# Splitting the first exponential of an attention chunk in two, so that the next projection waits for one bank

## The chip, the cores and the metric

The kernel runs on one core of one Trainium2 chip. The metric is the device time of one execution in microseconds (us). The core's engines run side by side, each through its own queue of instructions, and are ordered by semaphores alone: TensorE (PE; its weight loads are listed as PEld), ScalarE (ACT), VectorE (DVE), GpSimd (POOL) and SyncE (SP), which issues the DMAs here.

## The reference

One block of a perceiver, for four batches of 256 rows of width 256, in float32. Three steps, each added to its input: cross attention (16 heads of 64) of the rows on a context of 4096 keys of width 192; a gated linear recurrence; a mixture of eight experts, of which each row takes two. The change lies in the cross attention:

```python
q = (x @ Wq).reshape(b, n, h, d).transpose(0, 2, 1, 3)
k = (context @ Wk).reshape(b, -1, h, d).transpose(0, 2, 1, 3)
v = (context @ Wv).reshape(b, -1, h, d).transpose(0, 2, 1, 3)
sim = jnp.einsum('bhid,bhjd->bhij', q, k) * scale
attn = jax.nn.softmax(sim, axis=-1)
out = jnp.einsum('bhij,bhjd->bhid', attn, v)
```

## The kernel before, in words

**Pairs, quads, chunks.** Two heads (a pair) are worked on at once, one in each half of the 128 partitions; two pairs are a quad. There are 16 quads (four batches of four). A pair's 4096 keys are taken in 8 chunks of 512 (numbered s = 0 to 7), so a quad has 16 chunks (t = 0 to 15), and the whole cross attention 256. `CHUNK` gives their order and `T` numbers them from the start.

**What TensorE does in a chunk**, in the order of its queue (`quad` of `nc.Block.tensor`, from L386 on): for s = 0 the row maxima (`row_max`, L328) and the next pair's queries (`project_q`, L270); for some s a "guess" (L307), two matmuls of the next pair's scores in rough precision, from which DVE takes a maximum (`chunk_max`, L597); the chunk's scores, in two halves of 12 matmuls (L315, `hf` = 0 and 1), added onto banks which ACT has filled with the negated row maxima (`seed`, L482); in every s but 0 another guess; then one projection job out of a list written by hand (`JOBS`): 18 matmuls for keys (`project_k`, L279) or 36 for values (`project_v`, L290) of a later chunk, with a guess in its middle for s = 1 to 6; then the weighted sum of the values (`weighted_sum`, L323); for s = 2 the row sums (L332), for s = 3 the output projection (L337).

**The banks.** The scores of one half of a chunk take two PSUM banks, one per head: `score_bank(t, hf) = 2 * ((t + hf) % 2)` and the one after it. Banks 4 and 5 hold the guess (both at once, so a guess waits until DVE has taken the last one's maximum, `g_max`). Bank 6 (`psB`) and the first bank of this chunk's first half take the projection's two outputs, so the projection must wait until ACT has read that bank. Bank 7 holds the weighted sums.

**What ACT does in a chunk** (L508 on): the exponential of half 0, a 128x1024 activation over both banks of the half (`weights(0)`, L519 to L524), then that of half 1; a `seed` of the banks of half 1, which are those of the next chunk's half 0; for a key job two copies KH of 128x512 (`keys_hi`, L470) out of the projection's banks; and a `seed` of the banks of half 0, for the next chunk's half 1, once DVE has drained the projection out of them (`wait_drained`). For s = 0 it also copies the maxima (NM, L537) and scales the queries; after s = 7 it makes the diagonals (L477) from which `row_max` spreads the maxima.

**DVE and POOL.** DVE takes the maxima of guesses, drains the projections (KL, L578, after ACT's KH; V, L582), and once per pair inverts the row sums (L613); the guess number 6 waits for that. POOL adds the exponentials to `acc`, half by half (L717; L713 for the first).

**The semaphores.** `p_ready` counts exponentials, two per chunk. It is waited for by PE before the projection (L424) and before each half of the weighted sum, by ACT itself before each seed, and by POOL before each addition. The exponential itself waits for its scores (`s_ps`), for the last chunk's weighted sums (`pv_done`) and for POOL's addition of the same half a chunk ago (`acc_done`).

Of the kernel before, what the change touches and what calls it, by code (L numbers as in the profile page):

```python
# [7 lines left out]
ACT = mybir.ActivationFunctionType  # L8
# [18 lines left out]
def cross_attention(nc, nb, top, d):  # L27
# [4 lines left out]
    with ctx:  # L32
        def sb(name, shape, dt=F32):
            return ctx.enter_context(nc.sbuf_tensor(name, shape, dt))
# [12 lines left out]
        PR = sb("PR", [P, 2, 2, 2, ROWS])  # L47
# [32 lines left out]
        ps = ctx.enter_context(nc.psum_tensor("ps1", [P, 8, 512], F32))  # L80
# [18 lines left out]
        seeded, s_ps, p_ready, pv_done = sem("seeded"), sem("s_ps"), sem("p_ready"), sem("pv_done")  # L99
# [162 lines left out]
        def _(pe):  # L262
# [115 lines left out]
            def quad(it, b, g, last, final):  # L378
                for t in range(PER):
                    pi, s = t // NC, t % NC  # L380
                    p, T, c = it * 2 + pi, it * PER + t, CHUNK[t % NC]
                    nslot = 1 - pi
                    more = not (final and pi == 1)
                    rounds = ROUNDS[s] if more else (None, None, None)

                    def next_guess(n):  # L386
                        if n == 0:
                            pe.wait_ge(nm_sb, p + 1)
                            pe.wait_ge(q_ready, p + 2)
                        else:  # L390
                            pe.wait_ge(g_max, 16 * (p + 1) + n)
                        if n == 6:
                            pe.wait_ge(rl_ready, p + 1)
                        if n == 8:
                            pe.wait_ge(x_added, p + 2)
                        guess(p + 1, nslot, n)

                    if s == 0:
                        pe.wait_ge(m_diag, p + 1)
                        row_max()  # L400
                        if more:
                            pe.wait_ge(wq_in[nslot], (it + 1 + pi) * 16)
                            if last and pi == 1:
                                pe.wait_ge(xn_in, (b + 2) * 16)
                            project_q(nslot)
                    if rounds[0] is not None:
                        next_guess(rounds[0])
                    pe.wait_ge(k_lo, 2 * (4 * p + job_of(c)) + side_of(c) + 1)
                    for hf in range(2):
                        pe.wait_ge(seeded, 2 * T + hf + 1)  # L410
                        scores(pi, c, hf, score_bank(t, hf))
                    if rounds[1] is not None:
                        next_guess(rounds[1])
                    if has_job(t, final):
                        job = JOBS[t]
                        if t == 6:
                            pe.wait_ge(wk_in[0], 128 + 32 * (it + 1))
                        if t == 13:
                            pe.wait_ge(wk_in[1], 32 * (it + 2))
                        if t == 10:  # L420
                            pe.wait_ge(wv_in, 128 + 32 * (it + 1))
                        if last and job[0] == "K" and job[1] == 2:
                            pe.wait_ge(cready, b * 4 + 4 + job[2] + 1)
                        pe.wait_ge(p_ready, 2 * T + 1)  # L424
                        wait_drained(pe, it, t - 1, 1)
                        project(it, job, ps[:, score_bank(t, 0), :], psB,
                                (lambda: next_guess(rounds[2])) if rounds[2] is not None else (lambda: None))
                    elif rounds[2] is not None:
                        next_guess(rounds[2])
                    if pi == 0:  # L430
                        pe.wait_ge(v_sb, 2 * (8 * it + 2 * job_of(c) + 1) + side_of(c) + 1)
                    if s == 0:
                        pe.wait_ge(o_sb, p + 1)
                    for hf in range(2):
                        pe.wait_ge(p_ready, 2 * T + hf + 1)
                        mm = weighted_sum(pi, c, hf, s == 0, s == NC - 1)
                    mm.then_inc(pv_done, 1)
                    if s == 2:
                        pe.wait_ge(fold_done, p + 1)
                        if more:  # L440
                            pe.wait_ge(g_max, 16 * (p + 1) + 6)
                        row_sums()
                    if s == 3:
                        pe.wait_ge(ot_ready, p + 1)
                        pe.wait_ge(wo_in[nslot], (it + 1) * 32)
                        if more:
                            pe.wait_ge(g_max, 16 * (p + 1) + 8)
                        project_out(nslot)
# [11 lines left out]
        def _(act):  # L460
# [32 lines left out]
            for i, job in enumerate(FIRST_JOBS):  # L493
                if job[0] == "K":
                    n = 4 * job[1] + job[2]
# [14 lines left out]
            def quad(it, b, g, last, final):  # L510
                for t in range(PER):
                    pi, s = t // NC, t % NC
                    p, T = it * 2 + pi, it * PER + t
                    nslot = 1 - pi
                    more = not (final and pi == 1)
                    job = JOBS[t] if has_job(t, final) else None
                    banks = [score_bank(t, hf) for hf in range(2)]

                    def weights(hf):  # L519
                        act.wait_ge(s_ps, 2 * T + hf + 1)  # L520
                        act.wait_ge(pv_done, T + 1)
                        act.wait_ge(acc_done, 2 * T + hf + 1)
                        act.activation(PR[:, hf, :, :, :].rearrange("p h k n -> p (h k n)"),  # L523
                                       ps[:, banks[hf]:banks[hf] + 2, :].rearrange("p h n -> p (h n)"), ACT.Exp).then_inc(p_ready, 1)  # L524

                    if t == 0:
                        act.activation(warm[:], zero[:], ACT.Exp)
                    if s == 0:
                        act.wait_ge(nm_ps, p + 1)
                        row = psN.rearrange("p (h n) -> p h n", h=2)  # L530
                        seed(banks[0], row)
                        if has_job(t - 1, final):
                            wait_drained(act, it, t - 1, 0)
                        seed(banks[1], row)
                    weights(0)
                    if s == 0:
                        act.activation(NM[:, :, :].rearrange("p h n -> p (h n)"), psN, ACT.Copy).then_inc(nm_sb, 1)  # L537
                    weights(1)
                    if s == 0 and more:
                        act.wait_ge(q_ps, p + 2)  # L540
                        scale_q(nslot)
                    if s == NC - 1 and more:
                        act.wait_ge(m_ready, p + 2)
                        max_diagonals()
                    if s < NC - 1:
                        act.wait_ge(nm_sb, p + 1)
                        act.wait_ge(p_ready, 2 * T + 2)
                        seed(banks[1], NM[:, :, :])
                    if job is not None and job[0] == "K":
                        act.wait_ge(k_ps, k_num(it, job) + 1)  # L550
                        for side in range(2):
                            keys_hi(job[1] % 2, job[2], side, [ps[:, banks[0], :], psB][side])
                    if s < NC - 1:
                        if job is not None:
                            wait_drained(act, it, t, 0)
                        act.wait_ge(p_ready, 2 * T + 1)
                        seed(banks[0], NM[:, :, :])
                    if last and t in REFRESH:
                        j = REFRESH[t]
                        act.wait_ge(craw_in[0], 192 + (b * 4 + j + 1) * 64)  # L560

                        old_k, old_v = {0: (5, 2), 1: (6, 4), 2: (7, 6), 3: (8, 8)}[j]
                        act.wait_ge(k_ps, 8 * it + old_k)
                        act.wait_ge(v_ps, 8 * it + old_v)
                        context_hi(j, craw[:, :, :])
# [127 lines left out]
        def _(pool):  # L693
# [10 lines left out]
            def quad(it, b, g, last, final):  # L704
                for t in range(PER):
                    pi, s = t // NC, t % NC
                    p, T = it * 2 + pi, it * PER + t
                    flat = lambda a: a.rearrange("p h k n -> p (h k n)")
                    for hf in range(2):
                        pool.wait_ge(p_ready, 2 * T + hf + 1)  # L710
                        if s == 0 and hf == 0:
                            pool.wait_ge(fold_done, p + 1)
                            pool.tensor_tensor(flat(acc[:, :, :, :]), flat(PR[:, hf, :, :, :]),  # L713
# [749 lines left out]
```

## Time and profile before

| | us |
|---|---|
| median of 3 runs | 2403.74 |
| lowest and highest | 2401.39, 2408.85 |
| the profiled execution's own time | 2403.09 |
| its span, first to last instruction | 2401.3 |

The mean granted clock of TensorE in it is 0.976 of full speed. The cross attention is the first four fifths of the span. A row of a timeline gives the start and the duration in us, the engine and line, operation, output and inputs, how many instructions are merged in it, and in brackets how long the engine had been idle and what released it. Matmuls are pipelined: the duration of one runs into the next one's, so the time that PE spends on a stretch is read from starts, not from durations, and an idle time in brackets is counted from a modelled end.

### The profile page before, as it was taken

To read this page: it belongs to the slowest core of one execution; us is meant where nothing else is said; L and a number is where in the kernel's file an instruction comes from. 1 tells how busy PE (TensorE), PEld (TensorE's weight loads), DVE (VectorE), ACT (ScalarE), POOL (GpSimd) and SP (SyncE) were. 2 spreads that over 40 slices of the span, in tenths; PEclk is the share of its full clock that TensorE was granted. 3 is DMA by queue.
4 is the path that set the end of the run, shared out by engine and by line. 5 is a ranking of instruction groups with operands and counts; after the bars stand their busy time and mean duration, and the time that the engine had idled before them with its cause. 6 is when DMAs were issued, how large, how long until landed. Compare 5 with 4: busy or idle time off the path is not lost. (4 is left out here: it accounts for less than half of the span.)

```text
span 2401.3 us, 51408 instructions
## 1 busy us (share of the span) xinstructions
PE 2123.0 (88%) x19830; PEld 1549.2 (65%) x19830; DVE 1430.7 (60%) x1630; ACT 1347.4 (56%) x1657; POOL 1424.3 (59%) x651
## 2 busy tenths in 40 slices
PE   4899999889999998899999988999999968665998
PEld 3577767666767676667676766776777744224777
DVE  5655555555555555555555555555555525997586
ACT  2466666666666666666666666666666662001341
POOL 0366666666666666666666656666666770553364
PEclk9899999999999999999999999999999989998999
DMA  7010001110101011101000111010000002000230
GB/s 218 13 28 18 25 13 38 43 28 15 27 17 29 13 38 43 31 20 26 13 25 13 38 43 32 19 26 13 25 13 17 4 8 111 0 0 9 88 115 35
DMA packets 44521, 79.95 MB, mean 33 GB/s; under 512 B 7040, under 2 KB 31104, under 8 KB 43536
## 3 DMA queue, kind: packets, MB, share of 16 engines
q1 hardware_dynamic: 44304, 76.67, 11.2%
q8 instruction: 183, 3.00, 0.5%
q14 instruction: 34, 0.28, 0.0%
HBM read 69.90 MB, written 5.31 MB: 31 GB/s over the span
## 5 line engine op out<-in xcount | busy, mean ns | idle before, releaser
L717 POOL TENSOR_TENSOR acc<-acc,PR 128x1024 f32<-128x1024 f32 x480 | 1150.0, 2396 | 536.0 <-ACT PR L523 514.1
L597 DVE TENSOR_REDUCE amx<-ps 128x2 f32<-128x1024 f32 x512 | 627.7, 1226 | 440.3 <-PE ps L307 440.3
L523 ACT ACTIVATE PR<-ps 128x1024 f32<-128x1024 f32 x512 | 500.9, 1023 | 228.9 <-PE ps L315 225.2
L482 ACT ACTIVATE ps<-NM 128x1024 f32<-128x1024 f32 x448 | 461.4, 1031 | 276.6 <-DVE V L582 232.7
L323 PE MATMUL ps<-PR,V 128*64 128x256 f32 x4096 | 501.9, 387 | 5.7 <-ACT PR L523 5.5
L323 PEld LDWEIGHTS ps<-PR,V 128*64 128x64 f32 x4096 | 271.9, 137 | 182.4 <-issue 46.6
L290 PE MATMUL ps<-wv,C 64*128 64x256 f32 x4608 | 330.2, 286 | 34.2 <-ACT PR L523 32.3
L290 PEld LDWEIGHTS ps<-wv,C 64*128 64x128 f32 x4608 | 307.2, 189 | 70.8 <-issue 43.8
L279 PE MATMUL ps<-C,wk 64*128 64x512 f32 x2304 | 321.8, 408 | 29.6 <-ACT PR L523 17.0
L315 PE MATMUL ps<-qh,KH 64*128 64x256 f32 x2048 | 313.3, 301 | 8.6 <-ACT ps L482 8.1
L315 PE MATMUL ps<-ql,KH 64*128 64x256 f32 x2048 | 293.0, 281 | 0.0
L315 PE MATMUL ps<-qh,KL 64*128 64x256 f32 x2048 | 292.6, 281 | 0.0
L279 PEld LDWEIGHTS ps<-C,wk 64*128 64x128 f32 x2304 | 227.8, 191 | 89.0 <-issue 52.7
L307 PE MATMUL ps<-KH,qh 64*128 64x512 f32 x1024 | 233.3, 448 | 58.3 <-DVE amx L597 31.9
L315 PEld LDWEIGHTS ps<-qh,KH 64*128 64x128 f32 x2048 | 197.0, 188 | 74.6 <-issue 40.4
L578 DVE TENSOR_TENSOR KL<-ps,KH 128x512 fp32r<-128x512 f32 x256 | 165.0, 686 | 87.0 <-ACT KH L470 80.0
L315 PEld LDWEIGHTS ps<-ql,KH 64*128 64x128 f32 x2048 | 198.1, 189 | 4.3
L315 PEld LDWEIGHTS ps<-qh,KL 64*128 64x128 f32 x2048 | 198.2, 189 | 0.0
L470 ACT ACTIVATE KH<-ps 128x512 fp32r<-128x512 f32 x256 | 138.2, 591 | 100.0 <-PE ps L279 96.5
L307 PEld LDWEIGHTS ps<-KH,qh 64*128 64x128 f32 x1024 | 99.6, 186 | 126.5 <-issue 85.0
L582 DVE COPY V<-ps 128x512 f32<-128x512 f32 x256 | 163.9, 682 | 8.2 <-PE ps L290 8.1
L713 POOL TENSOR_TENSOR acc<-PR,zero 128x1024 f32<-128x1024 f32 x32 | 60.6, 1893 | 180.1 <-ACT PR L523 180.1
(164 smaller groups left out, 1747.4 us busy)
## 6 DMA issues: line engine op xcount, KB each, us to landing
wk<-wk_split SPq DMA_DIRECT2D x62, 192.0 KB, 3.2
wv<-wv_split SPq DMA_DIRECT2D x30, 384.0 KB, 5.1
bc<-wm_rows SPq DMA_DIRECT2D x16, 512.0 KB, 4.9
craw<-in_ctx SPq DMA_DIRECT2D x30, 256.0 KB, 3.8
we<-in_we SPq DMA_DIRECT2D x8, 768.0 KB, 7.6
wo<-in_wo SPq DMA_DIRECT2D x66, 64.0 KB, 2.2
wq<-in_wq SPq DMA_DIRECT2D x32, 128.0 KB, 2.4
craw<-in_ctx SPq DMA_DIRECT2D x30, 128.0 KB, 3.7
```

Of the source, the lines that this page charges most:

```text
L279: mm = pe.matmul(out, wk[half(h), slot, 3 * w + t, :], C[half(h), 3 * c + t, j * CH:j * CH + CH], start=(i == 0), stop=(i == len(PARTS) - 1))
L290: mm = pe.matmul(out[:, k * 256:k * 256 + 256], C[half(h), 3 * c + t, keys], wv[half(h), 3 * w + t, :], start=(i == 0 and k == 0), stop=(i ...
L307: mm = pe.matmul(ps[:, 4 + h, :], qh[half(h), slot, t * P:t * P + P], KH[half(h), slot, c, :], start=True, stop=True)
L315: mm = pe.matmul(ps[:, first_bank + h, k * ROWS:k * ROWS + ROWS], keys_of[half(h), slot, c, keys], q[half(h), slot, :], start=False, stop= ...
L323: mm = pe.matmul(psO[half(h), :], V[:, c * KT + 2 * hf + k, hd * DH:hd * DH + DH], PR[:, hf, h, k, :], start=(first and hf == 0 and k == 0 ...
L470: act.activation(KH[:, slot, j + 4 * side, :], bank, ACT.Copy).then_inc(k_hi, 1)
L482: act.activation(ps[:, first_bank:first_bank + 2, :].rearrange("p h (k n) -> p h k n", k=2), row.unsqueeze(2).to_broadcast([P, 2, 2, ROWS] ...
L523: act.activation(PR[:, hf, :, :, :].rearrange("p h k n -> p (h k n)"), ps[:, banks[hf]:banks[hf] + 2, :].rearrange("p h n -> p (h n)"), AC ...
L578: dve.tensor_tensor(KL[:, slot, c, :], bank, KH[:, slot, c, :].bitcast(F32), ALU.subtract).then_inc(k_lo, 1)
L582: dve.tensor_copy(V[:, k:k + 2, :].rearrange("p a n -> p (a n)"), bank).then_inc(v_sb, 1)
L597: dve.tensor_reduce(amx[:, :, t, c], psG, AX.X, ALU.max).then_inc(g_max, 1)
L717: pool.tensor_tensor(flat(acc[:, :, :, :]), flat(acc[:, :, :, :]), flat(PR[:, hf, :, :, :]), ALU.add).then_inc(acc_done, 1)
```

## The change

`weights(0)` becomes two activations of 128x512, head 0 (its bank is the one that the projection overwrites) and then head 1, each of which raises `p_ready`. The second half stays one activation. `p_ready` now grows by three per chunk. PE's projection waits for the first of the three; every other wait is renumbered and waits for as much as before.

```diff
@@ tensor
-                        pe.wait_ge(p_ready, 2 * T + 1)
+                        pe.wait_ge(p_ready, 3 * T + 1)
                         wait_drained(pe, it, t - 1, 1)
                         project(it, job, ps[:, score_bank(t, 0), :], psB,
@@ tensor, before the weighted sums
-                        pe.wait_ge(p_ready, 2 * T + hf + 1)
+                        pe.wait_ge(p_ready, 3 * T + hf + 2)
@@ scalar, weights(hf)
-                        act.activation(PR[:, hf, :, :, :].rearrange("p h k n -> p (h k n)"),
-                                       ps[:, banks[hf]:banks[hf] + 2, :].rearrange("p h n -> p (h n)"), ACT.Exp).then_inc(p_ready, 1)
+                        if hf == 0:
+
+                            for h in range(2):
+                                act.activation(PR[:, hf, h, :, :].rearrange("p k n -> p (k n)"), ps[:, banks[hf] + h, :], ACT.Exp).then_inc(p_ready, 1)
+                        else:
+                            act.activation(PR[:, hf, :, :, :].rearrange("p h k n -> p (h k n)"),
+                                           ps[:, banks[hf]:banks[hf] + 2, :].rearrange("p h n -> p (h n)"), ACT.Exp).then_inc(p_ready, 1)
@@ scalar, before the seeds
-                        act.wait_ge(p_ready, 2 * T + 2)
+                        act.wait_ge(p_ready, 3 * T + 3)
                         seed(banks[1], NM[:, :, :])
...
-                        act.wait_ge(p_ready, 2 * T + 1)
+                        act.wait_ge(p_ready, 3 * T + 2)
                         seed(banks[0], NM[:, :, :])
@@ gpsimd
-                        pool.wait_ge(p_ready, 2 * T + hf + 1)
+                        pool.wait_ge(p_ready, 3 * T + hf + 2)
```

## Rows read from the trace of the kernel before

**Rows 1.** Page, part 1: busy time, share of the span and instructions of each engine.

```profile
PE 2123.0 (88%) x19830; PEld 1549.2 (65%) x19830; DVE 1430.7 (60%) x1630; ACT 1347.4 (56%) x1657; POOL 1424.3 (59%) x651
```

**Rows 2.** Waits of PE: who waited for whom, us in total, times, longest us.

```profile
PE ps L290 <- ACT PR L523: 32.3, 90, 0.8
...
PE ps L279 <- ACT PR L523: 17.0, 58, 0.6
PE ps L279 <- issue: 10.6, 30, 0.4
```

**Rows 3.** Timeline of a chunk with a value job (t = 12, s = 4).

```profile
1017.68 1.94 ACT L523 ACTIVATE PR<-ps 128x1024 f32<-128x1024 f32 x2 [1.81 <-PE ps L315]
...
1018.07 0.39 PE L307 MATMUL ps<-KH,qh 64*128 64x512 f32 x2
...
1018.76 1.70 PE L290 MATMUL ps<-wv,C 64*128 64x256 f32 x24 [0.30 <-ACT PR L523]
...
1020.29 0.40 PE L307 MATMUL ps<-KH,qh 64*128 64x512 f32 x2
1020.53 0.89 PE L290 MATMUL ps<-wv,C 64*128 64x256 f32 x12
```

**Rows 4.** Timeline of a chunk with a key job (t = 13, s = 5).

```profile
1024.38 1.94 ACT L523 ACTIVATE PR<-ps 128x1024 f32<-128x1024 f32 x2 [0.76 <-PE ps L315]
...
1024.76 0.39 PE L307 MATMUL ps<-KH,qh 64*128 64x512 f32 x2
1025.19 1.23 DVE L597 TENSOR_REDUCE amx<-ps 128x2 f32<-128x1024 f32 x1 [2.04 <-PE ps L307]
...
1025.50 1.65 PE L279 MATMUL ps<-C,wk 64*128 64x512 f32 x12 [0.35 <-issue]
...
1026.96 0.42 PE L307 MATMUL ps<-KH,qh 64*128 64x512 f32 x2
...
1028.10 1.09 ACT L470 ACTIVATE KH<-ps 128x512 fp32r<-128x512 f32 x2 [0.66 <-PE ps L279]
...
1029.45 1.03 ACT L482 ACTIVATE ps<-NM 128x1024 f32<-128x1024 f32 x1 [0.27 <-DVE KL L578]
...
1030.68 0.28 PE L315 MATMUL ps<-qh,KH 64*128 64x256 f32 x2
```

**Rows 5.** Lines L523 and L470: duration in ns, least/median/longest, and first and last start.

```profile
L523 ACT ACTIVATE PR<-ps x512: 1000/1023/1040, 89.9 to 1965.4; 128x1024 f32<-128x1024 f32 x171
L470 ACT ACTIVATE KH<-ps x256: 569/592/601, 35.6 to 1899.7; 128x512 fp32r<-128x512 f32 x128
```

**Rows 6.** Timeline of PE: the first and the last open gap before a projection, of 209.

```profile
91.08 2.17 PE L290 MATMUL ps<-wv,C 64*128 64x256 f32 x32 [0.67 <-ACT PR L523]
...
1910.15 0.39 PE L307 MATMUL ps<-KH,qh 64*128 64x512 f32 x2
1910.72 1.69 PE L290 MATMUL ps<-wv,C 64*128 64x256 f32 x24 [0.17 <-ACT PR L523]
```

**Rows 7.** Timeline of a chunk with s = 3 (t = 11).

```profile
1010.63 0.50 PE L307 MATMUL ps<-KH,qh 64*128 64x512 f32 x2 [0.42 <-DVE rl L613]
...
1010.97 1.59 PE L290 MATMUL ps<-wv,C 64*128 64x256 f32 x24
```

**Rows 8.** Timeline from t = 8 (s = 0, a key job) into t = 9 (s = 1).

```profile
631.80 1.09 ACT L470 ACTIVATE KH<-ps 128x512 fp32r<-128x512 f32 x2
...
633.15 1.03 ACT L482 ACTIVATE ps<-NM 128x1024 f32<-128x1024 f32 x1 [0.27 <-DVE KL L578]
...
634.62 0.28 PE L315 MATMUL ps<-qh,KH 64*128 64x256 f32 x2
...
635.94 1.23 DVE L597 TENSOR_REDUCE amx<-ps 128x2 f32<-128x1024 f32 x1 [0.60 <-PE ps L307]
...
637.61 0.40 PE L307 MATMUL ps<-KH,qh 64*128 64x512 f32 x2
```

**Rows 9.** Waits of ACT, whole span: its seeds, for the row maxima at s = 0.

```profile
ACT ps L482 <- PE ps L328: 39.8, 30, 2.9
```

**Rows 10.** Timeline of POOL at the end of the cross attention, where there are no jobs.

```profile
1960.40 9.85 POOL L717 TENSOR_TENSOR acc<-acc,PR 128x1024 f32<-128x1024 f32 x4
```

## The prediction

> **What bounds the kernel now.** I read the page's busy times first: PE is busy for 2123.0 of 2401.3 us, the next engine for 1430.7 [rows 1]. So PE sets the pace, and what can be won is PE's idle time. PE's waits say where some of it lies: before a projection, for the exponential [rows 2]. The two lines put down to PR make 49.3 us in 148 waits; a third, "issue", 10.6 us in 30, has the same cause, since in a chunk of that kind the projection starts 1.12 us after the exponential, which takes 1.02 [rows 4, 5].
>
> The timelines show the wait, and that it is larger than its idle time. In the chunk of [rows 3] the exponential of half 0 starts at 1017.68; PE finishes the scores, starts a guess at 1018.07, then stands until the projection starts at 1018.76, that is 1.08 after the exponential's start and 0.69 after the guess. In the middle of the same projection a guess holds PE for no more than 0.24 (1020.29 to 1020.53). So PE could have gone on at 1018.31: the gap costs it 0.45, of which the record calls 0.30 idle, the rest being the modelled tail of the guess. In [rows 4] it is 0.74 after the guess, so 0.50 against 0.35 recorded. The two kinds alternate over the whole stage. Of its 246 projections I count 209 with such a gap between guess (or, at s = 0, last score matmul) and projection [rows 6]; 28 have none, nearly all at s = 3, where the guess itself is late, as it waited for the inverted row sums, and the projection follows at 0.34 [rows 7]; nine, in the quads that also refresh the context, start long after their exponential and wait for something else.
>
> **The change part by part.** *The first release comes earlier.* The trace holds no exponential of 128x512. The nearest row is ACT's copy of that shape, 592 ns; the exponential of 128x1024 is 1023 [rows 5]. I take 0.59, the shape being what sets it. The release moves from the 1.02 to the 0.59 of the exponential, by 0.43 us. From below, half of the long one would be 0.51 (a gain of 0.51); from above, a half costs as much as the whole, and the gain is nothing. I stay with the row of the same shape.
>
> *What PE makes of it.* Its gain in a chunk is the smaller of 0.43 and the gap less 0.24: in [rows 3] 0.43 against 0.45, in [rows 4] 0.43 against 0.50, in the last of [rows 6] 0.57 - 0.24 = 0.33. Worked out over the 209 gaps this sums to 88 us (0.42 each). The 28 and the nine give nothing.
>
> *What ACT pays.* Two copies of 128x512 back to back take 1.09, so the second starts 0.50 after the first; two exponentials take 1.94, so 0.92 apart [rows 3, 4]. The split first exponential then takes 0.50 + 0.50 = 1.00 to the next start where it took 0.92: everything behind it on ACT, the other exponential, the seed, the copies, comes 0.08 later. From above, with no overlap at all, it is 2 x 0.59 - 0.92 = 0.26; below nothing it can't be. In a key chunk ACT idles 0.66 before the copies KH, which PE releases [rows 4]. They come 0.43 earlier, ACT is ready 0.08 later: 0.15 are left, and 0.08 costs nothing. In a value chunk the second seed waits for DVE's copy and ACT has more room. POOL's two additions (2.4 each) start 0.07 later in chunks of 6 to 7 us, and nothing on PE waits for them.
>
> Where this cover is missing it is paid. At t = 8 (s = 0, with one more copy and a query scaling on ACT) KH starts with no idle time before it [rows 8]. There it will come 0.08 later and not 0.43 earlier, the seed behind it ends at 634.18 + 0.08, and the next scores' second half, at 634.62 - 0.43 = 634.19, waits some 0.12. Fifteen of these: 1.8 us.
>
> *The guess in the middle.* It needs DVE's maximum of the guess before. At s = 1 that ends at 635.94 + 1.23 = 637.17, and the guess, 637.61 before, would come at 637.18 [rows 8]; with some 0.06 to release it (so much lies between the exponential's end and the projection in [rows 3]), it is 0.05 late, in about 30 chunks: 1.5 us. At s = 5 it would come at 1026.53, the maximum ends at 1026.42 [rows 4]: just enough. So the new schedule runs into DVE's limit nearly exactly.
>
> *Does the shift last?* What follows the projection on PE (weighted sum, next scores) is already ready or hangs on the projection itself: KH, KL and the second seed. That chain, from the KH at 1028.10 to the seed's end at 1030.48, ends 0.20 before the scores that need it, at 1030.68 [rows 4]; all of it moves with the projection, so the 0.20 stays. At the start of a pair, PE's row maxima release ACT's seeds in 30 of 32 cases [rows 9], so PE's shift is passed on; in the two others it is lost: 0.8 us. The last ten chunks have no job and run at POOL's pace, four additions in 9.85 us [rows 10]; there the extra 0.07 counts about once. With what small things of this kind I can't see I set 0.5 for it.
>
> Sum: 88 - 1.8 - 1.5 - 0.8 - 0.5 = 83.4 us. The profiled execution took 2403.1 (span 2401.3 and 1.8 around it), which is 0.6 below the median of 2403.7. So 2403.1 - 83.4 + 0.6 = **2320**.
>
> **A rule against the change.** Two copies or exponentials of one ACT queue overlap by some 0.09 in the rows above, and I priced the split by that. The Trainium skill, "Advanced Engine Details and Errata", "The Read-Write Bubble", says the opposite for ScalarE: memory latency is exposed between instructions, so tiles should be large. This trace doesn't bear it out at 128x512. By the bubble the split's second instruction would pay its whole fixed part, which is the upper end of 0.26 above; the 0.15 of cover in key chunks would fall short by 0.11, still within the 0.20 before the scores, and t = 8 would pay 0.18 more, 2.7 us in all: 2323.
>
> **The rivals.** *The wait moves to DVE (about 2347).* The middle guess meets DVE's maximum with 0.05 to 0.1 to spare. If its release takes 0.10, as that of the projection in [rows 4], rather than 0.06, and PE restarts with a gap of 0.34 where an unbroken one takes 0.24, as it does after the late guess of [rows 7], a chunk loses up to 0.15 of its 0.42: 209 x 0.27 = 56 us, 2347. For it: the margins are that thin. Against: value jobs reach their middle guess later than key jobs do, 1.53 against 1.46 after their start [rows 3, 4]. Chance 0.20.
>
> *Nothing moves (2403).* The projection could be held by something else at nearly the same moment, another wait behind `p_ready` in PE's queue. Against it: the drain that it also waits for is that of the chunk before. Chance 0.04.
>
> *ACT becomes the bound, slower (about 2436).* If a half exponential costs as much as a whole one, the first release stays at 1.02 and all behind it comes 0.92 to 1.0 later. In a key chunk the 0.66 before KH and the 0.20 before the scores [rows 4] take 0.86 of 1.0: 0.14 to 0.2 late in some 100 key chunks, so 20 us; at t = 8, without the 0.66, 0.86 late fifteen times, 13 us. Together 33: 2436. It decides from an added cost of about 0.86 per chunk. Against it stands the 0.59 of [rows 5]. Chance 0.04.
>
> **How the numbers follow.** The forecast's own case gets 0.72. It spans 2303 (a half takes 0.51: 209 gaps then give up to 0.50, 104 us) to 2337 (0.34 instead of 0.42 in each gap, 71 less the 5 that are paid). The 8-in-10 range reaches over most of the DVE case: 2303 to 2360. About 7 us, 0.3%, is what a measurement of this kernel can tell from no change; the first two cases are faster by more (0.92), the third is no change (0.04), the last slower (0.04).
>
> **What would show it.** In the profile of the changed kernel: L523 with halves near 0.59, and the next exponential 1.0 after the first; the projection 0.65 to 0.75 after the first half's start instead of 1.08 to 1.16; the waits of PE for PR gone to a few us; PE's busy share up by some three points at nearly unchanged busy time; in their place a few us more of guesses waiting for DVE's maxima. The forecast is wrong if the projections do start earlier but the next chunk's scores do not (then the shift was lost on the way, and PE's waits name where), or if the halves take much longer than 0.59.

## The result, and the profile after

The changed kernel takes 2336.3 us (median of 4 runs, 2333.65 to 2340.31) against 2406.3 of the kernel before on the same chip (2401.39 to 2408.89). The ratio is 0.9713, with a 95% interval from 0.9690 to 0.9736: 69 us less, where 83 were forecast, inside the range. The profiled execution took 2333.65 us, its span is 2331.8 us and its granted clock 0.972.

The page's busy times after, and three of its groups (busy us, mean ns, idle before and its main releaser):

```profile
PE 2111.0 (91%) x19830; PEld 1539.4 (66%) x19830; DVE 1428.9 (61%) x1630; ACT 1363.6 (58%) x1913; POOL 1423.2 (61%) x651
...
L526 ACT ACTIVATE PR<-ps 128x512 f32<-128x512 f32 x512 | 277.7, 595 | 202.4 <-PE ps L315 185.8
L290 PE MATMUL ps<-wv,C 64*128 64x256 f32 x4608 | 328.0, 286 | 1.7 <-ACT PR L526 1.5
...
L279 PE MATMUL ps<-C,wk 64*128 64x512 f32 x2304 | 316.0, 404 | 0.0
```

PE's busy time is almost that of [rows 1], its share three points higher. ACT has 256 instructions and 16 us more. The 49.3 us in 148 waits and the 10.6 us of "issue" [rows 2] have become 1.7 us before value projections and nothing before key projections. What PE still waits for in this stage was mostly there before, somewhat larger at DVE's maxima (31.9 us in 18 waits before, as the same view of the kernel before has it). The third line is PE at the start of a quad, behind a turn of the program's loops; it was 20.5 in 10 before:

```profile
PE ps L307 <- DVE amx L602: 37.5, 19, 6.5
PE ps L307 <- DVE rl L618: 19.9, 30, 3.0
PE ps L328 <- issue: 19.8, 10, 2.3
```

The same two chunks as in [rows 3, 4], t = 12 and t = 13 of the same quad, in the timeline after:

```profile
983.82 1.09 ACT L526 ACTIVATE PR<-ps 128x512 f32<-128x512 f32 x2 [1.74 <-PE ps L315]
...
984.20 0.40 PE L307 MATMUL ps<-KH,qh 64*128 64x512 f32 x2
...
984.47 1.70 PE L290 MATMUL ps<-wv,C 64*128 64x256 f32 x24
...
990.10 1.08 ACT L526 ACTIVATE PR<-ps 128x512 f32<-128x512 f32 x2 [0.68 <-PE ps L315]
...
990.47 0.39 PE L307 MATMUL ps<-KH,qh 64*128 64x512 f32 x2
...
990.75 1.65 PE L279 MATMUL ps<-C,wk 64*128 64x512 f32 x12
...
991.07 1.03 ACT L528 ACTIVATE PR<-ps 128x1024 f32<-128x1024 f32 x1
...
993.42 1.09 ACT L470 ACTIVATE KH<-ps 128x512 fp32r<-128x512 f32 x2 [0.26 <-PE ps L279]
...
994.86 1.03 ACT L482 ACTIVATE ps<-NM 128x1024 f32<-128x1024 f32 x1 [0.35 <-DVE KL L583]
...
996.00 0.33 PE L315 MATMUL ps<-qh,KH 64*128 64x256 f32 x2
```

Each projection starts 0.65 after the exponential's start, where it was 1.08 and 1.12, and 0.27 to 0.28 after the guess. The period from one exponential's start to the next (983.82 to 990.10) is 6.28 where it was 6.70 (1017.68 to 1024.38).

I took this period, from the start of a chunk's first exponential to that of the next chunk's, for all 255 pairs of neighbours in both traces, and its median for each place t in a quad. This table shows where the time came from:

| t | before | after | difference |
|---|---|---|---|
| 0 | 6.81 | 6.44 | -0.37 |
| 1 | 6.93 | 6.72 | -0.21 |
| 2 | 7.21 | 6.95 | -0.26 |
| 3, 11 | 8.00, 8.03 | 8.01, 8.02 | 0.01, -0.01 |
| 4, 5, 6, 7 | 6.78, 6.69, 6.88, 8.06 | 6.35, 6.27, 6.48, 7.62 | -0.43, -0.41, -0.40, -0.44 |
| 8 | 6.71 | 6.29 | -0.42 |
| 9 | 6.93 | 6.83 | -0.10 |
| 10 | 7.31 | 6.95 | -0.36 |
| 12, 13, 14 | 6.69, 6.64, 7.01 | 6.26, 6.24, 6.58 | -0.43, -0.40, -0.43 |
| 15 | 10.03 | 9.47 | -0.56 |
| all 255 | 1873.8 | 1800.0 | -73.8 |

(At t = 15 the place ranges from 7.5 to 11.2 us from quad to quad; the median of the differences from chunk to chunk is -0.38 there, and -0.42 at t = 0.)

Eight places gave the full 0.40 to 0.45, the two at s = 3 nothing, as forecast. The shortfall sits at t = 1, 2 and 9, a little at 10, and in the three quads that refresh the context, where t = 5 gave nothing in all three and t = 7 in two. The chunks gave 73.8 us and the whole span 69.5: 1.6 more passed before the first exponential and 2.7 more behind the last chunk's first one. The program outside the chunks is the same in all kernels of this document, and from trace to trace that last part takes 437.6 to 443.8 us, so I don't put these 4 us down to the change.

### The profile page after: what moved, and what is told of

Its sections match the earlier page's. It is cut to its first block and busy times, and to the rows that moved or that the text cites. A ratio compares the mean times of both kernels' runs of the same rounds, so it can differ in the third digit from the quotient of the medians.

```text
span 2331.8 us, 52450 instructions
## 1 busy us (share of the span) xinstructions
PE 2111.0 (91%) x19830; PEld 1539.4 (66%) x19830; DVE 1428.9 (61%) x1630; ACT 1363.6 (58%) x1913; POOL 1423.2 (61%) x651
## 5 line engine op out<-in xcount | busy, mean ns | idle before, releaser
L526 ACT ACTIVATE PR<-ps 128x512 f32<-128x512 f32 x512 | 277.7, 595 | 202.4 <-PE ps L315 185.8
L279 PE MATMUL ps<-C,wk 64*128 64x512 f32 x2304 | 316.0, 404 | 0.0
L528 ACT ACTIVATE PR<-ps 128x1024 f32<-128x1024 f32 x256 | 265.0, 1035 | 3.3 <-POOL acc L722 3.3
L279 PEld LDWEIGHTS ps<-C,wk 64*128 64x128 f32 x2304 | 218.6, 189 | 47.5 <-ACT PR L526 5.9
L470 ACT ACTIVATE KH<-ps 128x512 fp32r<-128x512 f32 x256 | 138.7, 596 | 79.8 <-PE ps L279 76.5
```

What stands on the lines that cost most here:

```text
L279: mm = pe.matmul(out, wk[half(h), slot, 3 * w + t, :], C[half(h), 3 * c + t, j * CH:j * CH + CH], start=(i == 0), stop=(i == len(PARTS) - 1))
L526: act.activation(PR[:, hf, h, :, :].rearrange("p k n -> p (k n)"), ps[:, banks[hf] + h, :], ACT.Exp).then_inc(p_ready, 1)
```

## The experiments

"Changed kernel" below is the one after the change; each ratio is to the kernel before, measured beside it on the same chip. The periods and distances by place are medians, read from each run's timelines as for the table.

**The split alone.** The exponential stays split; the projection waits for both parts.

```diff
-                        pe.wait_ge(p_ready, 3 * T + 1)
+                        pe.wait_ge(p_ready, 3 * T + 2)
```

> The exponential is split, but the projection waits for both parts, so only the cost of the split is left of the change. My theory (parts overlap, 0.595 us each, the second starts 0.50 after the first): the full release comes 0.07 later than an undivided exponential's 1.02, in the 209 chunks where PE waits for it, so about 15 us slower than before (2421 against 2406), projections 1.23 after the exponential's start instead of 1.16. Rival, the parts do not overlap: 0.16 later, 33 us slower. Rival, a split is free: 2406.

Measured 2418.84 us, ratio 1.0040 (1.0027 to 1.0053): 10 us slower than before, where I expected 15. PE's waits for it, before value and key projections:

```profile
PE ps L290 <- ACT PR L526: 38.3, 103, 1.0
PE ps L279 <- ACT PR L526: 33.8, 102, 0.5
```

The projection starts 0.06 to 0.07 later after the exponential's start than before at most places (1.23 for 1.16 at t = 1, 1.14 for 1.08 at t = 12) and the periods there are 0.05 to 0.08 longer; at t = 3, 6, 11 and 13 they are unchanged, and at t = 10 0.05 shorter. (This kernel counts with 3T too, so what that costs, see the next run, is in its 10 us.) So a split costs what the overlap of its parts leaves, 0.07, not 0.16 and not nothing; the release is what brings the gain, some 80 us from here to the changed kernel (2418.84 and 2338.29 over nearly equal times of the kernel before, 2408.94 and 2409.46).

**A semaphore of its own for the first part.**

```diff
-                        pe.wait_ge(p_ready, 3 * T + 1)
+                        pe.wait_ge(p_first, T + 1)
...
-                                act.activation(PR[:, hf, h, :, :].rearrange("p k n -> p (k n)"), ps[:, banks[hf] + h, :], ACT.Exp).then_inc(p_ready, 1)
+                                act.activation(PR[:, hf, h, :, :].rearrange("p k n -> p (k n)"), ps[:, banks[hf] + h, :], ACT.Exp).then_inc(p_first if h == 0 else p_ready, 1)
...
-                        act.wait_ge(p_ready, 3 * T + 2)
+                        act.wait_ge(p_ready, 2 * T + 1)
                         seed(banks[0], NM[:, :, :])
```

(and the other waits back to 2T).

> As the changed kernel, but the first part raises a semaphore of its own and p_ready counts two per chunk again, so that its waits compare with 2T and not 3T. In the changed kernel ACT's second seed starts 0.35 after KL where it started 0.27 after it before. If the longer arithmetic of 3T on ACT's queue costs this 0.08, it is back at 0.27 here, the chunk t = 9 takes 0.08 less, and the time is 1 to 3 us under the changed kernel's 2336. Rival (the 0.08 is from something else, as a later release by DVE): 0.35 stays, and the time is within 1 us of it.

Measured 2333.15 us, ratio 0.9687 (0.9666 to 0.9708). The timeline of ACT from t = 8 into t = 9, first of the changed kernel, with its first exponential of t = 9:

```profile
722.12 1.13 ACT L470 ACTIVATE KH<-ps 128x512 fp32r<-128x512 f32 x2
...
723.59 1.03 ACT L482 ACTIVATE ps<-NM 128x1024 f32<-128x1024 f32 x1 [0.34 <-DVE KL L583]
...
724.85 1.09 ACT L526 ACTIVATE PR<-ps 128x512 f32<-128x512 f32 x2 [0.23 <-PE ps L315]
```

and of this kernel:

```profile
721.96 1.12 ACT L471 ACTIVATE KH<-ps 128x512 fp32r<-128x512 f32 x2
723.34 1.03 ACT L483 ACTIVATE ps<-NM 128x1024 f32<-128x1024 f32 x1 [0.27 <-DVE KL L584]
724.67 1.09 ACT L527 ACTIVATE PR<-ps 128x512 f32<-128x512 f32 x2 [0.30 <-PE ps L316]
```

The wait before the second seed is back at the 0.27 of [rows 4, 8], in every chunk with a key job, and t = 9 takes 6.78 instead of 6.83. So the 0.08 goes with counting by 3T, as expected. But it isn't the longer arithmetic: ACT's queue holds 2203 register, branch and semaphore instructions in both kernels, as in the kernel before. The changed kernel's own trace shows what it is, at the wait before this seed, L561 (ACT's queue, count, ns least/median/longest, first and last start), and in a row of its last quad:

```profile
L561 ACTq ALU_OP  x210: 35/35/35, 95.4 to 1794.5; - x105
L561 ACTq EVENT_SEMAPHORE  x6: 17/17/17, 1806.7 to 1840.0; - x6
...
1815.19 1.03 ACT L482 ACTIVATE ps<-NM 128x1024 f32<-128x1024 f32 x1 [0.27 <-DVE KL L583]
```

Inside the loops a register operation works out 3T + 2 there; it stands behind the wait for KL, runs only when KL is done (at 723.51 in the chunk above, with the seed at 723.59), and the seed follows it. In the last quad, which is outside the loops, the number to wait for is a constant, the operation is gone, and the same kernel has its 0.27, as the last row shows for t = 1. In the kernel before and in this one, the wait needs no new operation and is done with before KL comes. In the whole it is worth some 3 us by the medians, which the intervals of the two don't separate; the local reading does not hang on that.

**The middle guess later.** The changed kernel, with the guess in a projection one pair of matmuls later for keys, two for values.

```diff
-                    if i == 5:
+                    if i == 6:
                         middle()
...
-                        if k == 1 and i == 2:
+                        if k == 1 and i == 4:
                             middle()
```

> As the changed kernel, but the guess in the middle of a projection comes one pair of matmuls later in a key job and two later in a value job (0.24 to 0.27 us). Theory: at t = 1 and 9 that guess waits for DVE's maximum, which costs 0.19 in each (projection to weighted sum 2.68 instead of 2.50), and 0.05 at t = 2, 6, 10, 13; here these go, so 0.19 x 30 + 0.05 x 60 = 8 to 9 us less than the changed kernel: 2327. Rival: the later maximum delays DVE's copy of the projection and ACT's seed behind it, and the next scores wait instead: no gain, 2336 or more.

Measured 2318.76 us, ratio 0.9620 (0.9604 to 0.9636): some 18 us under the changed kernel's 2336.3 (19 to 22 by the ratios of its two measurements), twice what I expected. The changed kernel at t = 9:

```profile
725.49 0.40 PE L307 MATMUL ps<-KH,qh 64*128 64x512 f32 x2
...
725.72 1.55 PE L279 MATMUL ps<-C,wk 64*128 64x512 f32 x12
...
725.93 1.23 DVE L602 TENSOR_REDUCE amx<-ps 128x2 f32<-128x1024 f32 x1 [0.69 <-PE ps L307]
...
727.29 0.50 PE L307 MATMUL ps<-KH,qh 64*128 64x512 f32 x2
...
727.62 0.86 PE L279 MATMUL ps<-C,wk 64*128 64x512 f32 x6
...
728.40 1.95 PE L323 MATMUL ps<-PR,V 128*64 128x256 f32 x16
```

and this one, at the same place:

```profile
718.34 1.78 PE L279 MATMUL ps<-C,wk 64*128 64x512 f32 x14
...
718.55 1.23 DVE L602 TENSOR_REDUCE amx<-ps 128x2 f32<-128x1024 f32 x1 [0.70 <-PE ps L307]
...
719.94 0.47 PE L307 MATMUL ps<-KH,qh 64*128 64x512 f32 x2
...
720.24 0.63 PE L279 MATMUL ps<-C,wk 64*128 64x512 f32 x4
...
720.80 1.95 PE L323 MATMUL ps<-PR,V 128*64 128x256 f32 x16
```

In the first, DVE's maximum ends at 727.16, the guess can start only at 727.29, and the projection goes on 0.33 after it instead of 0.24; from the projection's start to the weighted sum it is 2.68. In the second DVE is done at 719.78, before the guess at 719.94, and it is 2.46, though the projection still goes on only 0.30 after the guess. By place the periods fall by 0.20 (t = 1), 0.13 (2), 0.22 (3), 0.06 (6), 0.23 (9), 0.15 (10), 0.15 (11), 0.05 (13): 1.19 per quad, 18 us over fifteen. What I had left out were t = 3 and 11, where the guess was late before the change too, and 0.08 to 0.10 at t = 2 and 10. No idle time of PE stands in the row of the late guess: the wait hides in the modelled tail of the matmul before it, which is why PE's waits hardly show it.

**The same edit without the split**, on the kernel before.

> The kernel before, undivided exponential, with the guess one or two pairs later and nothing else. Theory: DVE's limit at t = 1, 9 (0.19 each) and 2, 10 (0.05 to 0.14) was made by the earlier release, so only what t = 3 and 11 gave (0.21 and 0.15), where the guess before was late in both kernels, can come here: 0.36 x 15 = 5 us, 2403 against 2408. Rival, the later guess is better by itself everywhere, whatever the exponential does: 17 us, 2391.

Measured 2401.95 us, ratio 0.9966 (0.9952 to 0.9979), 7.5 us less. The periods of t = 3 and 11 fall by 0.19 and 0.16, which makes 5 of the 7.5; those of t = 1, 2, 9 and 10 change by 0.01 at most. So the edit is worth 18 us behind the split and 7.5 without it. The rest, some 10 us, is time that the earlier release ran into DVE's limit and lost again.

**One more copy on ACT**, behind the second exponential, in 7 of 8 chunks; nothing uses its result.

```diff
                     weights(1)
+                    if s > 0:
+                        act.wait_ge(padded, T + 1)
+                        act.activation(pad[:, :], NM[:, :, :].rearrange("p h n -> p (h n)"), ACT.Copy).then_inc(padded, 1)
+                    else:
+                        act.sem_inc(padded, 1)
```

> As the changed kernel, with one more copy of 128x512 on ACT behind the second exponential in 7 of 8 chunks (0.50 us each, 224 in all), whose result nothing uses. It asks how near ACT is to the bound. My theory: cover is left before KH (0.26 to 0.6 idle) and 0.12 before the next scores; only t = 6 and 13 are late, by some 0.12, so 4 us, at most 10, above the changed kernel's 2336. Rival, ACT has become the bound with the split: 0.50 x 200 = 100 us, 2436. Rival, ACT is covered wholly: 2336.

Measured 2337.66 us, ratio 0.9699 (0.9682 to 0.9716), within the changed kernel's spread. At t = 13 the idle time before KH goes from 0.26 to nothing and the period stays at 6.24; at t = 9 it goes from 0.60 to 0.25. The copy takes 0.35 more, not 0.50, since the seed behind it had waited some 0.15 for the exponential's end anyway. So no place was late; the bound rival is out, and ACT's cover held.

**Two such copies**, each waiting for the last.

> As the run with one added copy on ACT, but with two, each of which waits for the last, about 1.0 us more on ACT in 7 of 8 chunks. The changed kernel's cover, idle before KH plus margin before the next scores, is 0.85 at t = 1, 2.1 at t = 3, 0.62 at t = 6, 0.95 at t = 9, 0.38 at t = 13, and over 1.5 in value chunks. So 1.0 comes out late by 0.15, 0, 0.38, 0.05 and 0.62, 1.2 us per quad, 18 us in all, 2355. Rival, the cover is larger than read (as one copy cost less than I had set): under 2345. Rival, ACT's queue then bounds every chunk: over 2400.

Measured 2354.12 us, ratio 0.9767 (0.9752 to 0.9782): 16 us above the changed kernel, 18 expected. PE's waits for ACT's seeds:

```profile
PE ps L317 <- ACT ps L484: 23.3, 64, 1.2
```

were 8.3 us in 31 waits in the changed kernel. The lost time lies where the margins were read as smallest: one chunk behind t = 6 (t = 7, 7.89 for 7.62), at t = 13 (6.41 for 6.24) and behind it (t = 14, 7.07 for 6.58). t = 1 and 9 stay at 6.73 and 6.84. The two copies put the seed behind them 1.05 later (2.12 after the second exponential's start instead of 1.07), so the cover is some 0.4 us at t = 13 and 0.8 at t = 6; from there ACT decides.

**The changed kernel again, and both edits together.**

> The changed kernel itself once more, beside the kernels of this call: 2334 to 2340, P 0.71 to 0.73 of 3% under the kernel before, that is a ratio of 0.970 to 0.973.

> The changed kernel with both edits: a semaphore of its own for the first part, and the later guess in the middle. The two touch different waits (ACT's second seed, and DVE's maximum), so their gains add: 0.08 at t = 9 and at t = 8 from the first, the 17 us of the second: 2314 to 2318. If the later guess had used up what the own semaphore gives, 2319 as with the later guess alone.

Measured side by side: the changed kernel 2338.29 us, ratio 0.9699 (0.9682 to 0.9715); with both edits 2315.08 us, ratio 0.9607 (0.9594 to 0.9620). The intervals are apart: it beats both kernels, by 94 us the one before and by 23 us the changed one. t = 9 takes 6.53, against 6.60 with the later guess alone and 6.78 with the semaphore alone: there the two gains add. In the whole, the kernel with both edits and the one with the later guess alone (0.9604 to 0.9636) are not told apart.

## Why the prediction was right

**What bounds, and the first release.** Right, to the hundredth. I set a half exponential at 0.59 by the copy of the same shape [rows 5]; it takes 0.595. The release moved by 0.42 to 0.43 (1.08 to 0.65 at t = 12), and eleven places of sixteen (t = 0, 4 to 8, 10, 12 to 15) show 0.36 to 0.45 of it, t = 15 with 0.38 in its median difference from chunk to chunk. That gaps between starts, and not recorded idle times, are what a wait costs is borne out: the waits of [rows 2] add up to 60 us, and the time fell by 69.

**What ACT pays.** The cost was somewhat below what I set: the second exponential starts 0.97 after the first and not 1.00 (0.92 before). Inside the changed kernel it is hidden, as forecast; run alone, with the counting by 3T, it costs 10 us. The cover before KH was larger than worked out, 0.26 against 0.15, and the two runs with added copies show how far it reaches.

**The step that was mis-sized: the guess in the middle.** I had it 0.05 late at s = 1 only, for 1.5 us, and saw "just enough" elsewhere. At t = 1 and 9 the projection to weighted sum took 0.18 and 0.19 longer, at t = 2, 6, 10 and 13 0.04 to 0.07. Two things were missing in that term. At t = 1 and 9 the guess came 0.13 after DVE's end and not 0.06 (at t = 2 and 10 it is 0.06); and after a middle guess that waited, the projection goes on 0.33 later and not 0.24. I had the second number before me [rows 7] and used it only for the rival.

A guess that is late before the projection looks the same in the rows, but costs little. At t = 1, 2 and 10 the projection starts 0.33 or 0.34 after it, not 0.24. At t = 2 and 10 the first 24 matmuls of the projection then make up for it: the last of them starts 1.33 or 1.34 after the first, and not 1.42 as at t = 12 (at t = 1 only 0.03 comes back). With the later middle guess that gap is still 0.33, and t = 2 and 10 take 0.39 and 0.51 less than in the kernel before, where 0.40 and 0.43 were forecast. So in the changed kernel the time from guess to middle guess there, 1.82, is DVE's: its maximum ends 1.77 after the first guess.

The runs with the later guess put the loss at some 10 us of the 14 that the forecast was off. That is the DVE rival in part: its mechanism was there, in six places of sixteen. But at 2347 it was set too high by its own rule: it charged 0.15 in all 209 chunks, of which 58 (s = 0 and 7) have no middle guess, and should have read some 2339. The measured 2336 is nearer to that than to 2320, so the number by itself doesn't speak for the forecast; the periods by place do: t = 4, 5, 12 and 14, for which this rival takes 0.15 off too, gave 0.41 to 0.43. That the total came no nearer to 2320 has a part in it, some 4 us outside the chunks, that no run here explains.

*Slips that changed nothing.* With 0.26 for the split the cover before KH falls short by 0.03 and not by 0.11, since the 0.15 had 0.08 already taken off. And a gain of up to 0.50 in each of the 209 gaps adds up to 98 us and not 104, since many gaps are too short for it; the lower end would be near 2309.

**A small term missed.** "All of it moves with the projection, so the 0.20 stays": it became 0.12, since ACT's second seed now comes 0.08 later behind KL, for the register operation of 3T + 2. Beside the 0.05 of the split this made t = 8's late scores, which show in the period of t = 9. I had 1.8 us for that place; the split's own 0.05 and the seed's 0.08 together put the scores' second half at 724.67 in the quad shown, where the first half's start at 723.80 and the 0.71 between the two before give 724.51: 0.16 late, so 2.4 us.

**What is open.** In the refresh quads t = 5 gained nothing, and t = 7 nothing in two of three, where the other quads gave 0.41 and 0.44. These quads vary by several us between runs in which they should hardly differ (the one with the second refresh takes 128.2 before, 132.7 in the kernel before with the later guess, 133.6 in the split-alone run), and I made no run on them.

**The other rivals.** "Nothing moves" is out by the starts of the projections. "ACT becomes the bound" is out by the run with one added copy. The Trainium skill's "Read-Write Bubble" ("Advanced Engine Details and Errata") says that latency is exposed between instructions; it gives no figure. As the prediction read it, the split would have paid its fixed part in full, 0.26 to the next start; this trace shows 0.05, so at this shape most of that part lies under the instruction before.

## What to carry to other kernels

When an engine waits for an instruction of which it needs one part, split that instruction at a PSUM bank and let the part that is needed come first: here it moved the release by 0.43 us for 0.05 us on an engine with room. Then look at what the freed engine meets next: a margin of 0.05 us is not a margin, and moving the next wait by one pair of matmuls gave a quarter as much again. Keep the counters of the other waits as they were, with a semaphore of its own for the new event, or see to it that no register operation comes to stand between a wait and the instruction that it releases.

## What the runs showed that I had not expected

- Counting by 3T put a register operation between ACT's wait for KL and the seed, and with it 0.08 us (0.35 against 0.27), in every chunk with a key job inside the loops; a semaphore of its own took it away, and so does a constant in the last quad.
- A guess in the middle of a key projection that has waited for DVE costs twice on PE at t = 1 and 9: it starts 0.13 us after the release (0.06 in value projections), and the next group starts 0.33 us after it instead of 0.24. Neither stands as idle time in the records. The same 0.33 in front of the value projections at t = 2 and 10 cost nothing, as the projection gained it back.
- An ACT copy put between the exponential and the seed that waits for it cost 0.35 us and not its own 0.50, since the seed had waited 0.15 for the end of the exponential in any case.
- Where a loop of the program turns between two quads (10 of 15 times), the chunk t = 15 takes 9.85 to 11.23 us in the kernel before, and 7.92 to 7.97 where none does. PE's 20.5 us of waits before the row maxima (L328) are these ten. That is as much as the later guess gave, and no run here tried to win it.
